# Six channels instead of four per chunk in the inverse stages of a frequency-domain MLP

## Chip, cores and metric

One NeuronCore of one Trainium2 chip runs the whole program. The metric is the device time of one execution in microseconds. Lower is better. Three runs of the kernel before are shown, and one further execution was profiled.

## The reference

The input `x` has 4 images of 128 x 128 pixels with 768 channels (NHWC, float32). Each image goes through a real 2-D FFT, the channels are cut into 8 blocks of 96, every frequency of a block goes through two complex layers, and the result is transformed back and added to `x`:

```python
xf = jnp.fft.rfft2(x, axes=(1, 2), norm='ortho')            # B, H, 65, 8 blocks, 96
o1r = relu(xr @ w1[0] - xi @ w1[1] + b1[0])
o1i = relu(xi @ w1[0] + xr @ w1[1] + b1[1])
o2r = o1r @ w2[0] - o1i @ w2[1] + b2[0]
o2i = o1i @ w2[0] + o1r @ w2[1] + b2[1]
o = softshrink(stack([o2r, o2i]), 0.01)
out = jnp.fft.irfft2(complex(o), s=(H, W), axes=(1, 2), norm='ortho') + x
```

Here `@` is the product within a block. All of it is float32.

## The kernel before, in words

**Units.** The work is cut into 32 units, one for each image and block of 96 channels. All FFTs are matrix products. A unit runs on TensorE (`body`, line 970) as stages: A (the forward transform along width, line 831), B (first layer, lines 846 and 863), C (forward transform along height, line 877), D (second layer, lines 894 and 900), then the inverse: E (along height, line 916) and F (along width, lines 926 to 928). D seeds and shrinks pass through VectorE and ScalarE. TensorE's order is written out by hand: the layers of unit n, with the first two groups (`AHEAD`) of A of unit n+1 inside; the inverse of unit n; the other 22 groups of A of unit n+1; and then the last `LATE` chunks of F of unit n, at line 976, just before the layers of unit n+1.

**The inverse of a unit.** It goes in 24 chunks (`NQ`) of 4 channels (`CHUNK`). Per chunk:

- E (`stage_e`): 4 float32 products of 128x128 by 128x128, one for each channel, into one bank of PSUM (512 float32 per partition). The trace has two records for each float32 product, so 8 records for a chunk.
- High part (ScalarE, line 607): a copy of the bank into `sums_high`, rounded to fp32r, 128x512.
- Low part (VectorE, line 773): bank minus high part into `sums_low`, 128x512. It frees the bank and signals `low_copied`.
- F (`stage_f`): six fp32r products. The 128 rows are cut in two slots, `F_SLOTS`, of 65 and 63; each slot gets high x high, low x high and high x low weights. With 4 channels they have 260 and 252 columns, and one record each. All six write one bank.
- Add (VectorE, `add`, lines 763 and 767): 0.5 x the pixels plus the middle of F's bank (96 rows, 384 elements), then the 32 "spread" rows (128 elements). It signals `f_added`.

E rotates over three banks (4, 5, 6), F over three (0, 1, 7), and the high and low parts over `RING` = 4 buffers. TensorE and VectorE both go in batches of two chunks: E, E, then F, F of the batch before; VectorE low, low, then add, add of the batch before. E(q) waits for low(q-3), F(q) for low(q) and, from q = 3 on, for add(q-3). VectorE's and ScalarE's orders are fixed by hand too, and each queue is first in, first out.

**Ends of the inverse.** The first E waits for the last shrink (line 720) and for the copy of the flip. After the 22nd F comes A of the next unit in banks 4 to 7; ScalarE and VectorE then evict A's groups. Late F (chunks 22 and 23) writes banks 2 and 3. The first B product (line 846) waits for ScalarE's gather at line 505, which comes after the evictions at line 551.

Of the kernel before, what the change touches and what calls it, by code (L numbers as in the profile page):

```python
# [10 lines left out]
ALU = mybir.AluOpType  # L11
ACT = mybir.ActivationFunctionType

IMAGES, SIZE, HIDDEN, BLOCKS = 4, 128, 768, 8
BLOCK = HIDDEN // BLOCKS
# [5 lines left out]
FW_EVEN, FW_ODD, FH, IH, IH_FIRST, FLIP_RE, FLIP_IM, IW_COS, IW_SIN = (slice(SIZE * i, SIZE * (i + 1)) for i in range(9))  # L21
# [20 lines left out]
THIRD = BLOCK // 3  # L42
SPREAD = SIZE // 4
# [1 line left out]
A_ROWS = 4  # L45

NA = TILE_ROWS // A_ROWS
CHUNK = 4
NQ = BLOCK // CHUNK
RING = 4  # L50

BATCH = 2

LATE = 2
NF = NQ - LATE

F_SLOTS = [(0, HALF + 1), (HALF + 1, SIZE)]
# [11 lines left out]
def group_rows(t, b):  # L69

    if t < NP:
        return [12 * t + 3 * i + b for i in range(A_ROWS)]
    return [j if j < TILE_ROWS else MIDDLE for j in (12 * t + 3 * i + 3 - b for i in range(A_ROWS))]
# [91 lines left out]
def fourier_mlp(nc, x, w1, b1, w2, b2, dft, out):  # L165
    with ExitStack() as ctx:
        def sb(name, shape, dtype=F32):
            return ctx.enter_context(nc.sbuf_tensor(name, shape, dtype))

        def sem(name):  # L170
            return ctx.enter_context(nc.semaphore(name))
# [9 lines left out]
        U = spectrum[:, :].rearrange("p (s j) -> p s j", j=PITCH)  # L181
# [13 lines left out]

        sums_high, sums_low = (sb(f"sums_{x}", [SIZE, RING, SIZE, CHUNK], F32R) for x in ("high", "low"))
        doubled = sb("doubled", [SIZE, FOLD_ROWS, SIZE])
# [14 lines left out]
        psum = ctx.enter_context(nc.psum_tensor("psum", [SIZE, 8, 512], F32))  # L212

        def bank(i, p=SIZE, n=512):
            return psum[0:p, i, 0:n]

        E_BANKS, F_BANKS = 3, [0, 1, 7]

        AHEAD = 2

        def bank_a(at):

            return bank(2 + at if at < AHEAD else (4, 7, 5, 6)[(at - AHEAD) % 4])

        def banks_b(s):

# [35 lines left out]

        def bank_e(q):

            return bank(4 + q % E_BANKS).rearrange("p (c h) -> p h c", h=SIZE)

        def bank_f(q):

            return bank(F_BANKS[q % len(F_BANKS)] if q < NF else 2 + q - NF).rearrange("p (h c) -> p h c", c=CHUNK)

        def spread_sums(q):

            first = bank_f(q)[:, 0]
            return bass.AP(first.tensor, first.offset, [first.ap[0], [(SIZE - SPREAD // 2) * CHUNK, 2], [CHUNK, SPREAD // 2], [1, CHUNK]])

        def spread_part(t, q):

            b, c = divmod(q * CHUNK, THIRD)  # L280
            second = (MIDDLE, MIDDLE + 2, MIDDLE + 1)[b]
            first = t[:, b, BLOCK + c:BLOCK + c + CHUNK]
            return bass.AP(first.tensor, first.offset, [first.ap[0], [(second - b) * SIZE, 2], [3 * SIZE, SPREAD // 2], [1, CHUNK]])

        x_loaded = [[sem(f"x_loaded{i}_{p}") for p in range(NP)] for i in range(2)]
        half_set, x_halved = sem("half_set"), sem("x_halved")
# [19 lines left out]
        e_done, high_copied, low_copied = sem("e_done"), sem("high_copied"), sem("low_copied")  # L306
        f_done, f_added, f_late_added = sem("f_done"), sem("f_added"), sem("f_late_added")
# [51 lines left out]
        def pairs(s):  # L359
            return 1 if GROUPS[s][1] is None else 2  # L360
# [133 lines left out]
        def _(act):  # L494
# [109 lines left out]
            def inverse(n):  # L604
                for q in range(NQ):
                    act.wait_ge(e_done, n * NQ + (q + 1))
                    act.activation(sums_high[:, q % RING], bank_e(q), ACT.Copy).then_inc(high_copied, 1)  # L607

# [19 lines left out]
        def _(dve):  # L628
# [23 lines left out]
            def unfold_step(n, par, k):  # L652
# [3 lines left out]
                if k == 0:  # L656
                    dve.wait_ge(f_added, n * NF + NF)
                    dve.wait_ge(f_late_added, n * LATE + LATE)

# [98 lines left out]
            def add(par, n, q):  # L758

                x_unit = xs[par]  # L760
                dve.wait_ge(f_done, n * NQ + (q + 1))
                part = x_unit[:, :, q * CHUNK:(q + 1) * CHUNK]
                dve.scalar_tensor_tensor(part, part, 0.5, bank_f(q)[:, SPREAD // 2:SIZE - SPREAD // 2], op0=ALU.mult, op1=ALU.add)
                part = spread_part(x_unit, q)
                if q == 0:
                    dve.wait_ge(x_halved, n + 1)
                dve.tensor_tensor(part, part, spread_sums(q), ALU.add).then_inc(f_added if q < NF else f_late_added, 1)

            def inverse(par, n):
                for batch in range(0, NQ, BATCH):  # L770
                    for q in range(batch, batch + BATCH):
                        dve.wait_ge(high_copied, n * NQ + (q + 1))
                        dve.tensor_tensor(sums_low[:, q % RING], bank_e(q), sums_high[:, q % RING],  # L773
                                          ALU.subtract).then_inc(low_copied, 1)
                    for q in range(batch - BATCH, batch):
                        if q >= 0:
                            add(par, n, q)

            def forward_next(n, m, par):

# [22 lines left out]
            for q in range(NF, NQ):  # L803
                add(1, UNITS - 1, q)
# [4 lines left out]
        def _(pe):  # L809
            def mat(columns):  # L810
                return mats[:, columns]

            def stage_a(m, par, n, first, end, end_of=None):
                for at, g in list(enumerate(A_ORDER))[first:end]:
                    if at % (NA // NP) == 0:
                        pe.wait_ge(x_folded[par], m * NFOLD + 2 * (at // (NA // NP) + 1))
                    if at >= AHEAD + 4:

                        if at % 2 == 0:
                            pe.wait_ge(act_copied, n * ACT_COPIES + (at // 2 - 1))  # L820
                        else:
                            pe.wait_ge(dve_copied, n * DVE_COPIES + (at // 2 - 1))
                    elif end_of is not None and at == AHEAD + 1:

                        pe.wait_ge(f_added, end_of * NF + (NF - 1))
                    elif end_of is not None and at >= AHEAD:

                        pe.wait_ge(low_copied, end_of * NQ + (NQ - 2 if at == AHEAD else NQ + at - AHEAD - 3))
                    for i, j in enumerate(group_rows(*g)):

                        last = pe.matmul(bank_a(at)[:, i * SIZE:(i + 1) * SIZE], xs[par][:, j, :],  # L831
                                         mat(FW_EVEN if g[0] < NP else FW_ODD), start=i == 0, stop=True, skip_group_check=True)
                        if j == MIDDLE:
                            last = pe.matmul(bank_a(at)[0:BLOCK, i * SIZE:(i + 1) * SIZE], xs[par][:, j, 0:BLOCK],
                                             mat(FW_EVEN), start=True, stop=True)
                    last.then_inc(a_done, 1)
# [31 lines left out]
            def stage_c(n, s):  # L868
                pe.wait_ge(b_copied, n * NS + (s + 1))
                if s == 1:  # L870

                    pe.wait_ge(f_late_added, n * LATE)
                for i in range(pairs(s)):
# [35 lines left out]
            def stage_e(n, q):  # L909
                if q == 0:  # L910
                    pe.wait_ge(shrunk, n * NS + NS)
                    pe.wait_ge(flip_copied, n + 1)
                if q >= E_BANKS:
                    pe.wait_ge(low_copied, n * NQ + (q - E_BANKS + 1))
                for i in range(CHUNK):
                    last = pe.matmul(bank_e(q)[:, :, i], U[:, q * CHUNK + i, 4:], mat(IH_FIRST if q * CHUNK < THIRD else IH), start=True, stop=True)  # L916
                last.then_inc(e_done, 1)

            def stage_f(n, q):
                pe.wait_ge(low_copied, n * NQ + (q + 1))  # L920

                if len(F_BANKS) <= q < NF:
                    pe.wait_ge(f_added, n * NF + (q - len(F_BANKS) + 1))
                for j, (lo, hi) in enumerate(F_SLOTS):
                    high, low, out = sums_high[:, q % RING, lo:hi], sums_low[:, q % RING, lo:hi], bank_f(q)[:, lo:hi]
                    pe.matmul(out, iw_high[:, j], high, start=True, stop=False)  # L926
                    pe.matmul(out, iw_high[:, j], low, start=False, stop=False)  # L927
                    last = pe.matmul(out, iw_low[:, j], high, start=False, stop=True)  # L928
                last.then_inc(f_done, 1)
# [25 lines left out]
                    stage_a(*ahead, 1, AHEAD)  # L955

            def inverse(n):
                for batch in range(0, NQ, BATCH):
                    for q in range(batch, batch + BATCH):
                        stage_e(n, q)  # L960
                    for q in range(batch - BATCH, batch):
                        if q >= 0:
                            stage_f(n, q)

            def late(n):
                for q in range(NF, NQ):
# [40 lines left out]
```

## Time and profile before

| what | us |
|---|---|
| median of 3 runs | 4921.51 |
| lowest and highest run | 4920.08, 4923.3 |
| profiled execution, its own time | 4919.26 |
| its span | 4917.5 |
| TensorE matmul busy | 4843.5 (98%) |
| VectorE busy | 3747.3 (76%) |
| ScalarE busy | 3015.9 (61%) |
| GpSimd busy | 1562.1 (32%) |
| granted TensorE clock, mean | 0.996 |

The profile comes from one execution. Busy time of an engine is the time in which it executes at least one instruction; TensorE's products are pipelined, so that one record lasts about 0.28 us while the next starts about 0.11 us later. The distance between starts is what a product costs, and the duration is what the next engine waits for. Weight loads have records of their own (PEld) and lie beside the products.

### The profile page before, as it was taken

What the parts mean: (1) busy time and instruction counts of PE and PEld (TensorE: products, weight loads), DVE (VectorE), ACT (ScalarE), POOL (GpSimd) and SP (SyncE); (2) the same over time, 40 slices, a digit from 0 to 9 for tenths busy, and PEclk for the clock granted to TensorE, in tenths of its full rate; (3) what the DMA queues carried; (4) which work ended last, traced back from release to release, by engine and by line L of the source; (5) the groups of instructions that cost most, each with busy time, mean ns of one, the idle gap of its engine ahead of it and who ended that gap; (6) DMA issues with size and microseconds to landing.
All of it is one profiled execution on the core that took longest, in us unless ns stands there. A gap on an engine that the chain in (4) does not pass through costs nothing.

```text
span 4917.5 us, 113473 instructions
## 1 busy us (share of the span) xinstructions
PE 4843.5 (98%) x40000; PEld 4707.5 (96%) x40000; DVE 3747.3 (76%) x5948; ACT 3015.9 (61%) x5428; POOL 1562.1 (32%) x1098
## 2 busy tenths in 40 slices
PE   8999999999999999999999999999999999999996
PEld 7999999999999999999999999999999999999996
DVE  5777777777777777777777777777777777777776
ACT  6655666556665556665566655666556666556653
POOL 3043223433234332244322343233433234332230
PEclk9999999999999999999999999999999999999998
DMA  5044423444333443334432344423444333443333
GB/s 118 19 96 109 102 60 75 91 109 106 68 72 88 103 107 78 73 83 96 109 85 64 83 96 109 98 65 75 91 109 104 70 75 84 103 107 80 70 78 90
DMA packets 1699713, 430.24 MB, mean 87 GB/s; under 512 B 1698848, under 2 KB 1698976, under 8 KB 1699104
## 3 DMA queue, kind: packets, MB, share of 16 engines
q1 hardware_dynamic: 1696768, 421.83, 38.7%
q8 instruction: 345, 5.65, 0.5%
q14 instruction: 264, 2.16, 0.2%
q10 hardware_dynamic: 2336, 0.59, 0.1%
HBM read 220.84 MB, written 201.33 MB: 86 GB/s over the span
## 4 chain that ended last, share of the span: by engine, by line
PE 97%; ACT 1%; issue 1%; SPq 1%; DVE 1%; DMA 0%; DVEq 0%; ACTq 0%
PE psum L846 15%; PE psum L877 14%; PE psum L900 14%; PE psum L916 14%; PE psum L831 13%; PE psum L863 8%; PE psum L894 7%; PE psum L926 4%; PE psum L927 4%; PE psum L928 4%; SPq L395 1%; PE psum L907 0%; PE psum L906 0%; DVE x L669 0%; DVE x L664 0%
## 5 line engine op out<-in xcount | busy, mean ns | idle before, releaser
L607 ACT ACTIVATE sums_high<-psum 128x512 fp32r<-128x512 f32 x768 | 458.1, 598 | 725.5 <-PE psum L916 725.4
L567 ACT ACTIVATE excess<-psum,over 128x768 f32<-128x768 f32 (+1 forms) x544 | 481.5, 885 | 579.4 <-PE psum L900 543.8
L846 PE MATMUL psum<-w_whole,whole 128*128 128x192 f32 x4160 | 802.0, 335 | 14.2 <-ACT whole L515 11.0
L900 PE MATMUL psum<-w2t,hidden 128*128 128x192 f32 x4160 | 763.2, 327 | 0.0
L846 PEld LDWEIGHTS psum<-w_whole,whole 128*128 128x128 f32 x4160 | 680.6, 196 | 83.8 <-issue 66.1
L916 PE MATMUL psum<-mats,spectrum 128*128 128x128 f32 x6144 | 747.5, 276 | 3.9 <-DVE sums_low L773 2.9
L877 PE MATMUL psum<-mats,mixed 128*128 128x128 f32 x6272 | 750.2, 275 | 0.0
L712 DVE COPY mixed<-psum 128x768 f32<-128x768 f32 (+1 forms) x512 | 475.1, 928 | 354.4 <-PE psum L846 312.8
L877 PEld LDWEIGHTS psum<-mats,mixed 128*128 128x128 f32 x6272 | 739.9, 192 | 1.2
L831 PE MATMUL psum<-mats,x 128*128 128x128 f32 x6144 | 706.2, 276 | 19.9 <-DVE x L648 19.8
L720 DVE SCALAR_TENSOR_TENSOR spectrum<-psum,excess 128x768 f32<-128x768 f32 (+1 forms) x512 | 481.4, 940 | 316.9 <-ACT excess L567 316.9
L916 PEld LDWEIGHTS psum<-mats,spectrum 128*128 128x128 f32 x6144 | 714.5, 192 | 8.8 <-DVE sums_low L773 4.1
L831 PEld LDWEIGHTS psum<-mats,x 128*128 128x128 f32 x6144 | 699.2, 193 | 20.6 <-issue 16.3
L773 DVE TENSOR_TENSOR sums_low<-psum,sums_high 128x512 fp32r<-128x512 f32 x768 | 530.1, 692 | 241.7 <-ACT sums_high L607 241.7
L900 PEld LDWEIGHTS psum<-w2t,hidden 128*128 128x128 f32 x4160 | 688.4, 190 | 7.2 <-issue 7.2
L444 POOL TENSOR_TENSOR x<-x 128x192 f32<-128x192 f32 x31 | 15.7, 505 | 1833.2 <-DMA x<-x 1833.1
L447 POOL TENSOR_TENSOR doubled<-x 128x640 f32<-128x640 f32 (+1 forms) x248 | 369.1, 1488 | 536.6 <-DMA x<-x 523.1
L734 DVE COPY psum<-b_rows 128x768 f32<-128x768 f32 (+1 forms) x544 | 504.5, 927 | 1.1
L863 PE MATMUL psum<-w_halved,halved 64*128 64x192 f32 x4160 | 463.3, 339 | 0.0
L926 PE MATMUL psum<-sums_high,iw_high 128*128 128x260 f32 (+1 forms) x1536 | 462.0, 301 | 0.0
L453 POOL TENSOR_TENSOR x<-x,doubled 128x640 f32<-128x640 f32 (+1 forms) x248 | 444.6, 1793 | 17.0
L894 PE MATMUL psum<-w2t,middle 64*128 64x192 f32 x4160 | 448.6, 326 | 0.8 <-DVE middle L725 0.8
(81 smaller groups left out, 7451.1 us busy)
## 6 DMA issues: line engine op xcount, KB each, us to landing
x<-x SPq DMA_DIRECT2D x736, 192.0 KB, 2.8
out<-x SPq DMA_DIRECT2D x736, 192.0 KB, 2.4
x<-x SPq DMA_DIRECT2D x736, 64.0 KB, 2.6
out<-x SPq DMA_DIRECT2D x736, 64.0 KB, 2.2
x<-x SPq DMA_DIRECT2D x32, 144.0 KB, 2.6
out<-x SPq DMA_DIRECT2D x32, 144.0 KB, 2.3
w2t<-L_conv_w SPq DMA_DIRECT2D x124, 36.0 KB, 1.8
x<-x SPq DMA_DIRECT2D x64, 48.0 KB, 2.3
```

Source lines behind the costliest of these rows:

```text
L567: act.activation(excess[:, :, 0:rows_d(t)], parts_d(t), ACT.Relu, bias=over[:, 0:1]).then_inc(excess_done, 1)
L720: dve.scalar_tensor_tensor(dst, parts_d(t), LAMBDA, excess[:, :, 0:rows], op0=ALU.add, op1=ALU.min).then_inc(shrunk, 1)
L734: dve.tensor_copy(bank_d(s).rearrange("p (k r) c -> p k r c", r=2)[:, 0:k], b2_rows[par][:, :, :].unsqueeze(1).broadcast_to([SIZE, k, 2, B ...
L773: dve.tensor_tensor(sums_low[:, q % RING], bank_e(q), sums_high[:, q % RING], ALU.subtract).then_inc(low_copied, 1)
L831: last = pe.matmul(bank_a(at)[:, i * SIZE:(i + 1) * SIZE], xs[par][:, j, :], mat(FW_EVEN if g[0] < NP else FW_ODD), start=i == 0, stop=Tru ...
L846: last = pe.matmul(bank_b(s, k), whole[s % 2][:, k // 2, :, k % 2], w1_whole[par][:, :, :].rearrange("p r o -> p (r o)"), start=opens and ...
L863: last = pe.matmul(bank_b(s, i + 2 * y), halved[s % 2][rows, :, i], w1_halved[par][rows, :, :].rearrange("p r o -> p (r o)"), start=opens ...
L877: last = pe.matmul(out[tile], flat[:, tile * SIZE:(tile + 1) * SIZE], mat(FH), start=True, stop=True)
L894: pe.matmul(sums_d(s, i + 2 * y), middle[s % 2][rows, i], w2_tile(par, rows, 1), start=False, stop=False, skip_group_check=True)
L900: last = pe.matmul(sums_d(s, k), hidden[s % 2][:, k // 2, k % 2], w2_tile(par, slice(0, SIZE), 2 * (k // 2)), start=False, stop=True, skip ...
L916: last = pe.matmul(bank_e(q)[:, :, i], U[:, q * CHUNK + i, 4:], mat(IH_FIRST if q * CHUNK < THIRD else IH), start=True, stop=True)
L926: pe.matmul(out, iw_high[:, j], high, start=True, stop=False)
```

## The change

`CHUNK` goes from 4 to 6, so the inverse of a unit has 16 chunks instead of 24. An E chunk is 6 products and takes a pair of banks (4 and 5, or 6 and 7). F's two slots have 390 and 378 columns; the first ends where one bank ends and the second begins the next bank. All F chunks but the last use the pair 0 and 1; the last one (`LATE` = 1) uses 2 and 3. The high and low parts have `RING` = 3 buffers of 768 elements per partition. Batches go: TensorE issues E(q), then F(q-2), and VectorE low(q), then add(q-1). E(q) waits for low(q-2), F(q) for low(q) and add(q-1). The spread part of an add is cut in two where its six channels cross a third of the block (chunks 5 and 10). The order of A's banks is 4, 5, 6, 7 instead of 4, 7, 5, 6.

```diff
--- before.py
+++ after.py
@@ -45,13 +45,13 @@
 A_ROWS = 4
 NA = TILE_ROWS // A_ROWS
-CHUNK = 4
+CHUNK = 6
 NQ = BLOCK // CHUNK
-RING = 4
-BATCH = 2
-LATE = 2
+RING = 3
+LEAD = 2
+LATE = 1
 NF = NQ - LATE
 F_SLOTS = [(0, HALF + 1), (HALF + 1, SIZE)]
@@ -216,13 +216,11 @@
-        E_BANKS, F_BANKS = 3, [0, 1, 7]
         AHEAD = 2
         def bank_a(at):
-            return bank(2 + at if at < AHEAD else (4, 7, 5, 6)[(at - AHEAD) % 4])
+            return bank(2 + at if at < AHEAD else 4 + (at - AHEAD) % 4)
         def banks_b(s):
@@ -264,23 +262,32 @@
         def bank_e(q):
-            return bank(4 + q % E_BANKS).rearrange("p (c h) -> p h c", h=SIZE)
+            flat = psum[:, 4 + 2 * (q % 2):6 + 2 * (q % 2), :].rearrange("p y n -> p (y n)")
+            return flat[:, 0:CHUNK * SIZE].rearrange("p (c h) -> p h c", h=SIZE)
         def bank_f(q):
-            return bank(F_BANKS[q % len(F_BANKS)] if q < NF else 2 + q - NF).rearrange("p (h c) -> p h c", c=CHUNK)
-        def spread_sums(q):
-            first = bank_f(q)[:, 0]
-            return bass.AP(first.tensor, first.offset, [first.ap[0], [(SIZE - SPREAD // 2) * CHUNK, 2], [CHUNK, SPREAD // 2], [1, CHUNK]])
-        def spread_part(t, q):
-            b, c = divmod(q * CHUNK, THIRD)
+            first, lo = 0 if q < NF else 2, 512 - F_SLOTS[0][1] * CHUNK
+            flat = psum[:, first:first + 2, :].rearrange("p y n -> p (y n)")
+            return flat[:, lo:lo + SIZE * CHUNK].rearrange("p (h c) -> p h c", c=CHUNK)
+        def spread_channels(q):
+            lo, hi = q * CHUNK, (q + 1) * CHUNK
+            cut = [lo] + [c for c in range(THIRD, BLOCK, THIRD) if lo < c < hi] + [hi]
+            return list(zip(cut, cut[1:]))
+        def spread_sums(q, lo, hi):
+            first = bank_f(q)[:, 0, lo - q * CHUNK:hi - q * CHUNK]
+            return bass.AP(first.tensor, first.offset, [first.ap[0], [(SIZE - SPREAD // 2) * CHUNK, 2], [CHUNK, SPREAD // 2], [1, hi - lo]])
+        def spread_part(t, lo, hi):
+            b, c = divmod(lo, THIRD)
             second = (MIDDLE, MIDDLE + 2, MIDDLE + 1)[b]
-            first = t[:, b, BLOCK + c:BLOCK + c + CHUNK]
-            return bass.AP(first.tensor, first.offset, [first.ap[0], [(second - b) * SIZE, 2], [3 * SIZE, SPREAD // 2], [1, CHUNK]])
+            first = t[:, b, BLOCK + c:BLOCK + c + hi - lo]
+            return bass.AP(first.tensor, first.offset, [first.ap[0], [(second - b) * SIZE, 2], [3 * SIZE, SPREAD // 2], [1, hi - lo]])
         x_loaded = [[sem(f"x_loaded{i}_{p}") for p in range(NP)] for i in range(2)]
         half_set, x_halved = sem("half_set"), sem("x_halved")
@@ -761,20 +768,20 @@
                 dve.wait_ge(f_done, n * NQ + (q + 1))
                 part = x_unit[:, :, q * CHUNK:(q + 1) * CHUNK]
                 dve.scalar_tensor_tensor(part, part, 0.5, bank_f(q)[:, SPREAD // 2:SIZE - SPREAD // 2], op0=ALU.mult, op1=ALU.add)
-                part = spread_part(x_unit, q)
                 if q == 0:
                     dve.wait_ge(x_halved, n + 1)
-                dve.tensor_tensor(part, part, spread_sums(q), ALU.add).then_inc(f_added if q < NF else f_late_added, 1)
+                for lo, hi in spread_channels(q):
+                    part = spread_part(x_unit, lo, hi)
+                    added = dve.tensor_tensor(part, part, spread_sums(q, lo, hi), ALU.add)
+                added.then_inc(f_added if q < NF else f_late_added, 1)
             def inverse(par, n):
-                for batch in range(0, NQ, BATCH):
-                    for q in range(batch, batch + BATCH):
-                        dve.wait_ge(high_copied, n * NQ + (q + 1))
-                        dve.tensor_tensor(sums_low[:, q % RING], bank_e(q), sums_high[:, q % RING],
-                                          ALU.subtract).then_inc(low_copied, 1)
-                    for q in range(batch - BATCH, batch):
-                        if q >= 0:
-                            add(par, n, q)
+                for q in range(NQ):
+                    dve.wait_ge(high_copied, n * NQ + (q + 1))
+                    dve.tensor_tensor(sums_low[:, q % RING], bank_e(q), sums_high[:, q % RING],
+                                      ALU.subtract).then_inc(low_copied, 1)
+                    if 1 <= q <= NF:
+                        add(par, n, q - 1)
             def forward_next(n, m, par):
@@ -820,12 +827,9 @@
                             pe.wait_ge(act_copied, n * ACT_COPIES + (at // 2 - 1))
                         else:
                             pe.wait_ge(dve_copied, n * DVE_COPIES + (at // 2 - 1))
-                    elif end_of is not None and at == AHEAD + 1:
-                        pe.wait_ge(f_added, end_of * NF + (NF - 1))
                     elif end_of is not None and at >= AHEAD:
-                        pe.wait_ge(low_copied, end_of * NQ + (NQ - 2 if at == AHEAD else NQ + at - AHEAD - 3))
+                        pe.wait_ge(low_copied, end_of * NQ + (NQ - 1 if at < AHEAD + 2 else NQ))
                     for i, j in enumerate(group_rows(*g)):
                         last = pe.matmul(bank_a(at)[:, i * SIZE:(i + 1) * SIZE], xs[par][:, j, :],
@@ -910,17 +914,17 @@
                 if q == 0:
                     pe.wait_ge(shrunk, n * NS + NS)
                     pe.wait_ge(flip_copied, n + 1)
-                if q >= E_BANKS:
-                    pe.wait_ge(low_copied, n * NQ + (q - E_BANKS + 1))
+                if q >= 2:
+                    pe.wait_ge(low_copied, n * NQ + (q - 1))
                 for i in range(CHUNK):
-                    last = pe.matmul(bank_e(q)[:, :, i], U[:, q * CHUNK + i, 4:], mat(IH_FIRST if q * CHUNK < THIRD else IH), start=True, stop=True)
+                    last = pe.matmul(bank_e(q)[:, :, i], U[:, q * CHUNK + i, 4:], mat(IH_FIRST if q * CHUNK + i < THIRD else IH), start=True, stop=True)
                 last.then_inc(e_done, 1)
             def stage_f(n, q):
                 pe.wait_ge(low_copied, n * NQ + (q + 1))
-                if len(F_BANKS) <= q < NF:
-                    pe.wait_ge(f_added, n * NF + (q - len(F_BANKS) + 1))
+                if 1 <= q < NF:
+                    pe.wait_ge(f_added, n * NF + q)
                 for j, (lo, hi) in enumerate(F_SLOTS):
                     high, low, out = sums_high[:, q % RING, lo:hi], sums_low[:, q % RING, lo:hi], bank_f(q)[:, lo:hi]
                     pe.matmul(out, iw_high[:, j], high, start=True, stop=False)
@@ -955,12 +959,11 @@
                     stage_a(*ahead, 1, AHEAD)
             def inverse(n):
-                for batch in range(0, NQ, BATCH):
-                    for q in range(batch, batch + BATCH):
+                for q in range(NF + LEAD):
+                    if q < NQ:
                         stage_e(n, q)
-                    for q in range(batch - BATCH, batch):
-                        if q >= 0:
-                            stage_f(n, q)
+                    if q >= LEAD:
+                        stage_f(n, q - LEAD)
             def late(n):
                 for q in range(NF, NQ):
```

## Rows read from the trace of the kernel before

**Rows 1.** The page: busy time of each engine, and the chain that ended last by engine.

```profile
PE 4843.5 (98%) x40000; PEld 4707.5 (96%) x40000; DVE 3747.3 (76%) x5948; ACT 3015.9 (61%) x5428; POOL 1562.1 (32%) x1098
...
PE 97%; ACT 1%; issue 1%; SPq 1%; DVE 1%; DMA 0%; DVEq 0%; ACTq 0%
```

**Rows 2.** Critical chain, a unit's inverse and after; columns start us, us, what.

```profile
148.19 1.78 PE psum L916 x16
...
173.74 1.78 PE psum L916 x16
...
176.94 19.69 PE psum L831 x176
...
208.75 1.30 PE psum L900 x8
```

**Rows 3.** Timeline of TensorE, three F triples of unit 0; columns start, duration, engine, line.

```profile
143.78 0.27 PE L926 MATMUL psum<-sums_high,iw_high 128*128 128x252 f32 x1
...
144.13 0.28 PE L926 MATMUL psum<-sums_high,iw_high 128*128 128x260 f32 x1
...
144.49 0.28 PE L926 MATMUL psum<-sums_high,iw_high 128*128 128x252 f32 x1
...
144.73 1.87 PEld L916 LDWEIGHTS psum<-mats,spectrum 128*128 128x128 f32 x16
144.84 1.95 PE L916 MATMUL psum<-mats,spectrum 128*128 128x128 f32 x16
```

**Rows 4.** Timeline of TensorE, the last two F triples of either width.

```profile
4881.09 0.28 PE L926 MATMUL psum<-sums_high,iw_high 128*128 128x252 f32 x1
...
4881.44 0.29 PE L926 MATMUL psum<-sums_high,iw_high 128*128 128x260 f32 x1
...
4881.80 0.28 PE L926 MATMUL psum<-sums_high,iw_high 128*128 128x252 f32 x1
```

**Rows 5.** Groups by line and shape: busy us, mean ns of one, idle before.

```profile
L773 DVE TENSOR_TENSOR sums_low<-psum,sums_high 128x512 fp32r<-128x512 f32 x768 | 530.1, 692 | 241.7 <-ACT sums_high L607 241.7
...
L607 ACT ACTIVATE sums_high<-psum 128x512 fp32r<-128x512 f32 x768 | 458.1, 598 | 725.5 <-PE psum L916 725.4
...
L720 DVE SCALAR_TENSOR_TENSOR spectrum<-psum,excess 128x768 f32<-128x768 f32 x480 | 457.1, 952 | 298.4 <-ACT excess L567 298.4
...
L567 ACT ACTIVATE excess<-psum,over 128x768 f32<-128x768 f32 x480 | 432.1, 900 | 504.2 <-PE psum L900 468.5 <-DVE spectrum L720 34.7
L763 DVE SCALAR_TENSOR_TENSOR x<-x,psum 128x384 f32<-128x384 f32 x768 | 419.6, 546 | 1.0
...
L557 ACT ACTIVATE hidden<-psum,b1t 128x256 f32<-128x256 f32 x512 | 242.1, 473 | 243.9 <-PE psum L877 243.9
...
L767 DVE TENSOR_TENSOR x<-x,psum 128x128 f32<-128x128 f32 x768 | 215.5, 281 | 0.0
```

**Rows 6.** Timeline of all engines where the inverse of unit 0 starts.

```profile
138.94 0.76 DVE L720 SCALAR_TENSOR_TENSOR spectrum<-psum,excess 128x576 f32<-128x576 f32 x1 [2.19 <-ACT excess L567]
...
139.75 2.87 PEld L916 LDWEIGHTS psum<-mats,spectrum 128*128 128x128 f32 x25
...
140.95 0.60 ACT L607 ACTIVATE sums_high<-psum 128x512 fp32r<-128x512 f32 x1 [1.65 <-PE psum L916]
141.58 0.69 DVE L773 TENSOR_TENSOR sums_low<-psum,sums_high 128x512 fp32r<-128x512 f32 x1 [1.88 <-ACT sums_high L607]
```

**Rows 7.** Critical chain at the end of the last unit: VectorE's adds back to back.

```profile
4881.49 0.46 DVE x L763
4881.96 0.20 DVE x L767
```

**Rows 8.** Busy time in one stretch of the inverse: PE, PEld, DVE, ACT, POOL, clock.

```profile
145.00:176.00 31.00, 31.00 (x275) 31.00 (x274) 26.29 (x59) 11.79 (x20) 0.00 (x0) 1.00 0.07 12
```

**Rows 9.** Timeline of ScalarE and TensorE where late F ends and B starts.

```profile
197.62 0.33 ACT L505 ACTIVATE whole<-spectrum 96x132 f32<-96x132 f32 x1
...
197.99 1.29 PEld L846 LDWEIGHTS psum<-w_whole,whole 128*128 128x128 f32 x8 [0.16 <-ACT whole L505]
```

## Prediction

> **What bounds the kernel now.** I read the page first. TensorE is busy 98% of the span and makes 97% of the chain that ended last; VectorE, ScalarE and GpSimd are busy 76%, 61% and 32% [rows 1]. So only two things change the time: what TensorE's own records cost, and gaps put between them. Busy time of the other engines matters only where TensorE must wait for it. The busy times by stretch show the inverse at its densest: in 31 us TensorE is busy for all 31.00, VectorE for 26.29, ScalarE for 11.79, GpSimd for none, at a granted clock of 1.00, which is 2.4 GHz [rows 8]. VectorE has the least slack there.
>
> The critical chain prices TensorE's records by the distance from one to the next. 16 E records (two E chunks of 4 channels) take 1.78 us, 0.1115 each. From the batch that ends its E at 148.19 + 1.78 to the one at 173.74 there are 8 batches in 25.55 us, 3.194 each [rows 2]; what is left for 12 F records is 1.41 us, 0.1177 each, 0.707 for an F chunk. F has on average 256 columns, 0.1067 us at 2.4 GHz, so an F record costs 11 ns above its columns.
>
> The timeline at the start of an inverse gives the latencies between engines. The first E's load starts 0.05 us after VectorE's shrink has ended (138.94 + 0.76, then 139.75). A load leads its product by 0.11 us (144.73 and 144.84 [rows 3]), so the first E takes effect at 139.86. Its 8 records are through at 140.75 and ScalarE starts at 140.95: 0.20 us from TensorE's last record to a waiting engine. VectorE starts 0.03 us after ScalarE ends [rows 6].
>
> **The change, part by part.** The profiled execution took 4919.26 us (span 4917.5), 2.2 under the median of 4921.51; the sum is made against the former and 2.2 added.
>
> *F's records.* Before, 22 chunks stand in the inverse: 22 x 0.707 = 15.55 us a unit. The new chunk has three records of 390 columns (162.5 ns) and three of 378 (157.5 ns), together 0.960 us, plus the six surcharges. At 11 ns each that is 1.026 us, and 15 chunks are 15.39: a gain of 0.16 us a unit. No row shows an fp32r record so long, so the surcharge is bounded. From below: a D record of 192 columns streamed twice (384) takes 1.30 / 8 = 0.1625 us [rows 2], only 2.5 ns over its 160. With that the chunk is 0.975 and the gain 0.93. From above: cost in proportion, 1.5 x 0.707 = 1.061, is a loss of 0.36. Steeper still, three F records of 252 columns take 0.35 us and three of 260 take 0.35 to 0.36 (first and last of 385 of each; their means are 0.346 and 0.360) [rows 3, 4]; drawn out from 8 columns to 130 more, that slope makes the chunk 1.14 and loses 1.6, which I leave outside the range. I take the fixed 11 ns, since it belongs to the same kind of record and the slope speaks against the cheaper one.
>
> The Trainium skill ("TensorE: Matmul & The Clock Gate", Back-to-back issue gap) gives N / 2.4 + 2.5 ns for a warm product. By that page F gains about 25 us over the kernel. The D record agrees with it, F before, at 11, doesn't.
>
> *Late F* shrinks from two chunks (1.41 us) to one (1.03). It frees nothing. The first B product already waits 0.16 us there for ScalarE's gather, which ends at 197.95, and its load starts at 197.99 [rows 9]; that chain starts from A's last groups, not from F. The wait grows to about 0.5 us, in place of F's 0.38. Cost 0. The shorter late add on VectorE, and A's new bank order, also cost 0: A's evictions cover them.
>
> *E* has the same 192 records, 21.4 us a unit. One chunk takes 12 x 0.1115 = 1.34 us.
>
> *High, low, add for six channels.* High: a copy of 512 takes 598 ns; ScalarE's slope from 256 (473) to 768 elements (900) is 0.834 ns each, so 768 take about 0.81 us, and at most the 0.90 of line 567. Low: 692 ns for 512 and 1.04 ns for each further element, 0.96, which the 952 of line 720 (768 elements in two banks) bears out [rows 5]. Add: VectorE starts the spread part 0.46 us after the main part and the next instruction 0.20 later [rows 7]. With 192 and 64 more elements the main part takes 0.46 + 0.20 = 0.66 and the spread part lasts 0.281 [rows 5] + 0.07 = 0.35: 1.01 us. In chunks 5 and 10 the split adds one start, 0.07. VectorE's total in a chunk of 2.37 us is 0.96 + 0.66 + 0.27 = 1.9, so it isn't full. ScalarE (0.81) hides. Reading two banks is what lines 720 and 567 do now. Nothing in the DMA queues moves, SP and POOL have no new step.
>
> *New wait 1, at E(2).* It needs low(0), where before E(3) did. From E(0) in effect at 139.86 in that unit: E(0) through at 141.20, high from 141.40 to 142.21, low from 142.24 to 143.20, load 143.25, product 143.36. E(1) is through at 142.54. **0.82 us** of TensorE idle. Behind it in the queue stand F(0) and everything else.
>
> *New wait 2, at F(14).* F has one pair of banks, so F(q) waits for add(q-1). After E(15) there is no E left: F(13), then F(14) at once. From F(13)'s end: 0.20 to VectorE, 1.01 for the add, 0.05 to the load, 0.11 to the product: **1.37 us** idle. Before, three banks took F(20) and F(21) without it.
>
> *New wait 3, at F(1) to F(13).* The same 1.37 us stands beside one E chunk of 1.34. Short by 0.03, 13 times, and by 0.07 more in the two split chunks: **0.53 us** a unit. Bounds: none, if the overlap is a few hundredths better; 0.9, if it is 0.03 worse each time. Low(q) behind add(q-2) on VectorE isn't late: from F(q-2)'s end it is done after 0.20 + 0.66 + 0.27 + 0.96 = 2.09 us, and E(q+2)'s load wants it after 1.37 + 1.03 - 0.11 = 2.29.
>
> The sum a unit: 0.82 + 1.37 + 0.53 - 0.16 = 2.56 us. In 32 units 81.9: 4919.3 + 81.9 + 2.2 = **5003 us**.
>
> What could hide these waits? Only idle in front of TensorE later in the unit, and that is the 0.16 us at B [rows 9], which comes from a chain counted from A and moves with it.
>
> **The rivals.** (a) F's surcharge falls to 2.5 ns. For it: the D record [rows 2]. Against it: F's own surcharge and slope [rows 3, 4]. 0.77 us a unit less, 5003 - 25 = 4978. The waits stay.
>
> (b) Wait 3 is larger: VectorE's round trip of 1.37 us is built from five short pieces, and 0.1 us more on it costs 13 x 0.1 x 32 = 42: 5045. VectorE's rows of 546 and 281 ns are steady, which speaks against it; that no row shows VectorE released by F does not exclude it.
>
> (c) The other side: faster. The mechanism is that an F record is paced by its weight load and not by its columns, so that wider records come free: 0.1177 us stay 0.1177, 15 chunks take 10.6, a gain of 4.9 a unit against 2.7 of waits: 5003 - 151 = 4852. The point from which it decides: F's chunk must fall under (15.55 - 2.72) / 15 = 0.855 us, 0.143 a record, while 390 columns alone are 0.1625 at the full clock and D's 384 cost just that. Very unlikely.
>
> (d) The waits don't appear, because bank or buffer reuse doesn't bind: then 5003 - 87 = 4916, within the noise of no change. The code names both semaphores and the rows have the durations, so hardly.
>
> **How the numbers follow.** About 0.2%, 10 us, is what a measurement here can tell from no change. Forecast 0.62, (a) 0.22, (b) 0.11, (c) 0.03, (d) 0.02. The range: down by (a), 25, and no wait 3, 17, to 4962; up by F in proportion, 17, high at 0.90, 3, and wait 3 at its bound, 12, to 5035, which I cut to 5032. Faster by over 0.2% is (c), 0.03; within 0.2% is (d), 0.02; slower 0.95.
>
> **What the profile afterwards would show.** TensorE idle before line 916 released by VectorE's line 773, once a unit, 0.8 us. Idle before line 926 released by line 767, once a unit 1.4 us and up to 13 times a few hundredths. F records 0.173 and 0.168 us apart; 0.165 and 0.160 mean (a). High 0.81, low 0.96, add's main part 0.75 and spread part 0.35 us. Line 846 waiting about 0.5 us for line 505. TensorE's share lower, the clock still 1.00. The prediction is wrong if line 926 is never released by VectorE, or if idle at line 926 in mid-inverse is over 0.1 us each.

## The result and the profile after

The changed kernel takes 5012.8 us (median of 4 runs, 5010.5 to 5014.9) against 4920.8. The ratio is 1.0188, with a 95% interval of 1.0175 to 1.0200. The change is slower, as forecast (5003 us, range 4962 to 5032), by 92 us in place of 82. The profiled execution took 5012.32 us with a span of 5010.1.

The page of the changed kernel, engines and chain, answers to [rows 1]:

```profile
PE 4876.9 (97%) x38464; PEld 4719.4 (94%) x38464; DVE 3683.8 (74%) x5244; ACT 2974.0 (59%) x5172; POOL 1554.4 (31%) x1098
...
PE 93%; ACT 2%; issue 2%; DVE 1%; SPq 1%; DMA 0%; ACTq 0%; DVEq 0%
```

TensorE has 1536 records fewer (38464; F's six per chunk, eight chunks fewer, in 32 units), yet it is busy 33 us longer and fills 97% of the span in place of 98%. Its share of the chain falls from 97% to 93%. The granted clock is still 1.00 in the inverse and 0.997 in the mean.

The groups by line and shape (busy us, mean ns of one, idle before) answer to [rows 5]. Lines 781, 614, 770 and 775 were 773, 607, 763 and 767:

```profile
L781 DVE TENSOR_TENSOR sums_low<-psum,sums_high 128x768 fp32r<-128x768 f32 x512 | 487.3, 952 | 93.9 <-ACT sums_high L614 93.8
...
L614 ACT ACTIVATE sums_high<-psum 128x768 fp32r<-128x768 f32 x512 | 416.3, 813 | 807.6 <-PE psum L920 807.6
...
L770 DVE SCALAR_TENSOR_TENSOR x<-x,psum 128x576 f32<-128x576 f32 x512 | 386.5, 755 | 295.1 <-PE psum L932 294.1
...
L775 DVE TENSOR_TENSOR x<-x,psum 128x192 f32<-128x192 f32 x448 | 155.9, 348 | 0.0
```

Low takes 952 ns (0.96 expected), high 813 (0.81), the add's main part 755 and its spread part 348. VectorE now waits 294 us in all for F at line 770; the same line had 1.0 us of waiting before [rows 5].

The waits (who waited for whom: us in total, times, longest):

```profile
DVE x L770 <- PE psum L932: 294.1, 480, 1.9
...
PE psum L930 <- DVE x L775: 35.9, 32, 1.2
...
PE psum L920 <- DVE sums_low L781: 19.8, 32, 1.1
```

TensorE waits once a unit at E (line 920) for a low part and once a unit at F (line 930) for an add. The totals, 19.8 and 35.9 us, understate these two: a record goes on for 0.16 us or more after the next one could have started, and that much of each gap is booked as busy. The critical chain shows them whole. First the start of the inverse of unit 0 (columns: start, duration, what):

```profile
140.63 1.51 PE psum L920 x12
...
142.16 0.82 ACT sums_high L614
...
143.01 0.97 DVE sums_low L781
143.98 0.04 issue
144.02 1.60 PE psum L920 x12
```

E(0)'s last record ends at 142.14 and ScalarE starts at 142.16; then come high 0.82, low 0.97, and E(2)'s load at 144.02. Its product takes effect 0.11 us later, at 144.13. E(0) took effect at 140.64 (its last record's end, less the record's 0.275 and eleven distances of 0.1115), so two chunks were through at 143.32: a gap of 0.81 us (0.82 in the forecast).

Then the middle of the inverse, one period:

```profile
149.11 1.34 PE psum L920 x12
150.45 0.22 PE psum L930
150.67 0.18 PE psum L931
150.85 0.18 PE psum L932
151.03 0.18 PE psum L930
151.21 0.17 PE psum L931
151.38 0.17 PE psum L932
151.55 1.34 PE psum L920 x12
```

One period is 151.55 - 149.11 = 2.44 us. The first of F's six records takes 0.22 us and the others 0.17 to 0.18. The timeline of the same place shows why:

```profile
151.21 0.33 PE L932 MATMUL psum<-sums_high,iw_low 128*128 128x378 f32 x1
...
151.58 0.76 DVE L770 SCALAR_TENSOR_TENSOR x<-x,psum 128x576 f32<-128x576 f32 x1 [0.55 <-PE psum L932]
...
152.25 0.35 DVE L775 TENSOR_TENSOR x<-x,psum 128x192 f32<-128x192 f32 x1
...
152.66 0.19 PEld L930 LDWEIGHTS psum<-sums_high,iw_high 128*128 128x128 f32 x1
```

F(2)'s last record ends at 151.54, VectorE starts at 151.58, its spread part ends at 152.60, and the load of F(3) starts 0.06 us after that. The low part that F(3) also needs, low(3), stands before this add in VectorE's queue, so it is the add that F(3) waits for last. No row of the waits names this: the gap is shorter than what a record's end hides. It can be read only from the distance between records.

And the end of the inverse:

```profile
178.24 0.18 PE psum L932
...
178.45 0.06 DVE x L770
...
179.12 0.36 DVE x L775
...
179.52 0.45 PE psum L930
```

F(13)'s last record ends at 178.42. F(14)'s load starts at 179.52, when the add is done. Unhindered, F(14)'s first record would have ended at 178.60; it ended at 179.52 + 0.45 = 179.97. That is a gap of 1.37 us, with no E left to fill it.

From the first E of unit 0 to that of unit 1 the kernel before takes 151.12 us (139.86 to 290.98) and the changed one 154.14 (140.63 to 294.77): 3.02 us a unit, and the inverse itself 40.21 in place of 37.08, 3.13 more.

### The profile page after: what moved, and what is told of

Read it like the earlier page. It is cut to its first block, busy times and chain, and to the rows that moved or that the text cites. A ratio compares the mean times of both kernels' runs of the same rounds, so it can differ in the third digit from the quotient of the medians.

```text
span 5010.1 us, 108315 instructions
## 1 busy us (share of the span) xinstructions
PE 4876.9 (97%) x38464; PEld 4719.4 (94%) x38464; DVE 3683.8 (74%) x5244; ACT 2974.0 (59%) x5172; POOL 1554.4 (31%) x1098
## 4 chain that ended last, share of the span: by engine, by line
PE 93%; ACT 2%; issue 2%; DVE 1%; SPq 1%; DMA 0%; ACTq 0%; DVEq 0%
PE psum L850 15%; PE psum L881 14%; PE psum L904 14%; PE psum L920 13%; PE psum L835 12%; PE psum L867 8%; PE psum L898 7%; PE psum L930 4%; PE psum L932 3%; PE psum L931 3%; DVE sums_low L781 1%; ACT spectrum L551 1%; ACT spectrum L558 1%; SPq L402 1%; ACT sums_high L614 1%
## 5 line engine op out<-in xcount | busy, mean ns | idle before, releaser
L614 ACT ACTIVATE sums_high<-psum 128x768 fp32r<-128x768 f32 x512 | 416.3, 813 | 807.6 <-PE psum L920 807.6
L920 PE MATMUL psum<-mats,spectrum 128*128 128x128 f32 x6144 | 769.2, 276 | 20.8 <-DVE sums_low L781 19.8
L920 PEld LDWEIGHTS psum<-mats,spectrum 128*128 128x128 f32 x6144 | 747.4, 191 | 30.5 <-DVE sums_low L781 25.8
L770 DVE SCALAR_TENSOR_TENSOR x<-x,psum 128x576 f32<-128x576 f32 x512 | 386.5, 755 | 295.1 <-PE psum L932 294.1
L781 DVE TENSOR_TENSOR sums_low<-psum,sums_high 128x768 fp32r<-128x768 f32 x512 | 487.3, 952 | 93.9 <-ACT sums_high L614 93.8
L455 POOL TENSOR_TENSOR x<-x 128x640 f32<-128x640 f32 (+1 forms) x248 | 454.7, 1833 | 0.0
```

## The experiments

Two theories stood against each other. One is the ledger: three separate waits and dearer F records, each with its own price. The other is the rival: the loss is in the two-bank chunks or the change of order as such, or the waits only hand their time on, so that removing one brings nothing. The base is the changed kernel (5012.8 us) unless another is named, and the unit's length is read as above.

**1. F(14) later.** TensorE issues F(14) behind the next unit's A groups 2 and 3, which need only low(14). The cut below is TensorE's part. VectorE does its add after the evictions of groups 1 and 3.

```diff
-                stage_a(m + par, 1 - par, n + 1, AHEAD, NA, end_of=n)
+                stage_a(m + par, 1 - par, n + 1, AHEAD, AHEAD + 2, end_of=n)
+                stage_f(n, NF - 1)
+                stage_a(m + par, 1 - par, n + 1, AHEAD + 2, NA, end_of=n)
```

> The changed kernel, with F(14) put behind the next unit's A groups 2 and 3 on TensorE, and its add on VectorE put behind the evictions of A groups 1 and 3. If the wait at F(14) is a cost of its own (1.37 us a unit): it disappears in 31 units, 5013 - 42 = 4971 us. If it only moves (VectorE's evictions come late and A group 7 waits for its bank): 0.5 to 1.4 us a unit come back there, 4985 to 5013.

Measured: 4977.1 us, ratio to the kernel before 1.0118 (1.0101 to 1.0135). That is 36 us less. The critical chain, where the inverse ends:

```profile
179.08 1.78 PE psum L837 x16
180.86 0.18 PE psum L932
...
181.92 15.37 PE psum L837 x136
```

The two A groups (16 records in 1.78 us) cover the add's round trip, and F(14)'s first record takes 0.18 us, the same as its neighbours: the gap is gone. From F(13) to F(14) and A the unit gains 1.37 us. But the unit is 152.93 us long, 1.21 less and not 1.37. The other 0.16 comes back inside A: its 136 records take 15.37 us, where 152 took 16.98 in the changed kernel, 0.1117 each, so that 15.19 was to be expected. VectorE now has the add between its evictions, which would make the next of them later. That this is the cause was not shown; it fits experiment 5, where the shorter add takes the 0.16 away. So the ledger holds here, and a tenth of the gain is handed on.

**2. Adds without their spread part** (line 775 is left out; the 32 spread rows get no sum).

```diff
-                for lo, hi in spread_channels(q):
-                    part = spread_part(x_unit, lo, hi)
-                    added = dve.tensor_tensor(part, part, spread_sums(q, lo, hi), ALU.add)
```

> The changed kernel without the spread part of the adds (32 of the 128 rows of a pixel column block get no sum). If F(1) to F(13) wait because VectorE's add is slightly longer than one E chunk: the add's signal comes 0.26 us earlier, the 13 waits (0.6 us a unit together) go and the one at F(14) falls from 1.37 to 1.1, in all 0.85 us a unit, 5013 - 27 = 4986 us. If low(q), queued behind the add, is what E and F really wait for in mid-inverse, or if these gaps are only the cost of going from E to F records: nothing of the 0.6, and 5013 - 8 = 5005.

Measured: 4978.1 us, ratio 1.0117 (1.0101 to 1.0134); 35 us less in place of 27. The unit is 153.20 us long, 0.94 less. One period in mid-inverse:

```profile
150.19 1.34 PE psum L917 x12
151.52 0.18 PE psum L927
...
152.58 1.34 PE psum L917 x12
```

The period is 2.39 us and the first F record takes 0.18. Over twelve periods the mean is 2.389 (147.80 to 176.47), against 2.441 in the changed kernel (146.69 to 175.98, with both split chunks): 0.052 us, 13 times, is 0.68 us a unit. The wait at F(14) fell by 0.26 (its total in the waits from 35.9 to 27.5 us, in 32 units). Together that is 0.94, all that this unit gained, and 30 of the 35 us over 32 units; some 3 more lie in the last four units (see "The sum" below). The run alone would not tell add from low, since without the spread parts low comes earlier too. The place does: the gap stood before F's first record and not before E's, and F(q) finds low(q) done before add(q-1). The add's round trip was the wait.

**3. High and low of chunk 0 in two pieces.** The first four channels go through ScalarE and VectorE while E still works on the last two. TensorE's and ScalarE's parts of the edit are shown; VectorE's is like ScalarE's.

```diff
+                    if q == 0 and i == 3:
+                        last.then_inc(e_part, 1)
...
+                    if q == 0:
+                        act.wait_ge(e_part, n + 1)
+                        act.activation(sums_high[:, 0, :, 0:4], bank_e(0)[:, :, 0:4], ACT.Copy).then_inc(high_part, 1)
+                        act.wait_ge(e_done, n * NQ + 1)
+                        act.activation(sums_high[:, 0, :, 4:], bank_e(0)[:, :, 4:], ACT.Copy).then_inc(high_copied, 1)
+                        continue
```

> The changed kernel, with the high and low parts of chunk 0 taken in two pieces (channels 0 to 3 after E's fourth product, then 4 and 5). If E(2) waits for the round trip through ScalarE and VectorE: low(0) ends at 2.75 + 0.1 us after E(0) starts and not at 3.34, the wait shrinks from 0.82 to 0.22 us a unit, 5013 - 19 = 4994 us. If the next wait (E(3) for low(1), or F(0)) takes it over: 5013.

Measured: 4997.0 us, ratio 1.0154 (1.0137 to 1.0171), 16 us less. The chain at the start:

```profile
139.75 4.42 PE psum L933 x36
144.17 0.18 PE psum L945
...
145.22 1.34 PE psum L933 x12
```

36 E records now run as one group of 4.42 us, with no step through ScalarE or VectorE between them. 36 x 0.1115 and the 0.16 us that a last record lasts on would be 4.17, so 0.25 us of waiting is left. The unit is 153.56 us, 0.58 less (0.60 expected). E(3) and F(0) don't take the wait over.

**4. Both edits, 1 and 3.** No new lines.

> The changed kernel with F(14) moved behind two groups of A and chunk 0 in two pieces, both edits of the two runs before together. If the waits at F(14) and at E(2) are separate costs: 5013 - 36 - 16 = 4961 us. If one covers for the other: 4975 to 4980.

Measured: 4960.8 us, ratio 1.0084 (1.0067 to 1.0101). The two are separate costs, and they add up as expected. This is the best version with six channels and all of the computation, and it is still 41 us slower than the kernel before.

**5. All three edits** (the spread part of the adds left out).

> Both edits, and the spread part of the adds left out, so that F never waits for an add. If the ledger is complete: 4961 - 13 x 0.052 x 32 = 4939 us, still above the kernel before by F's dearer records (0.24 us a unit), 0.25 at E(2) and 0.16 in A, 21 in all. If records of 390 and 378 columns were a gain that the waits hid: below 4920.

Measured: 4929.6 us, ratio 1.0021 (1.0011 to 1.0030), 9 us better than expected and still above the kernel before. The chain at the end of the inverse:

```profile
173.58 1.34 PE psum L932 x12
...
175.97 1.78 PE psum L847 x16
...
178.81 15.20 PE psum L847 x136
```

The period is 2.39 us as in experiment 2. A's 136 records take 15.20 us: the 0.16 that came back in experiment 1 is gone too, probably because VectorE, without the spread parts, is earlier at its evictions (0.16 x 31 = 5 us of the 9). Another 3 us lie in the last four units: there a unit took 0.9 us more than elsewhere in experiment 4 and takes 0.1 more here (see "The sum" below). The unit is 151.53 us, 0.41 above the kernel before. F's records account for 0.24 of it and the rest of the wait at E(2) for 0.25, less 0.11 by which the part of the unit outside its inverse is shorter. Without any wait on an add, with less work on VectorE, the six-channel version doesn't win: the waits hid no gain.

**6. The order alone.** The kernel before, with three banks each for E and F and four channels, but in the new order without batches.

```diff
-                for batch in range(0, NQ, BATCH):
-                    for q in range(batch, batch + BATCH):
-                        stage_e(n, q)
-                    for q in range(batch - BATCH, batch):
-                        if q >= 0:
-                            stage_f(n, q)
+                for q in range(NQ):
+                    stage_e(n, q)
+                    if q >= 2:
+                        stage_f(n, q - 2)
```

VectorE's loop is changed in the same way.

> The kernel before (4 channels, three banks each for E and F), with the order of the changed one: TensorE E(q), F(q-2), VectorE low(q), add(q-2), no batches. If the loss comes from the number of banks and the size of the chunks: as the kernel before, 4920 us, within 10. If going from E to F records after every chunk has a price of its own (0.05 us twice as often as before would be 24 x 0.05 x 32 / 2 = 19): 4935 to 4945.

Measured: 4922.3 us over 10 runs, ratio 1.0005 (0.9995 to 1.0014): no difference that the times show. In the traces a unit takes 151.20 us in place of 151.12. So going from E to F after each chunk costs next to nothing, 0.08 us a unit. What is left for the loss is the size of the chunks and the number of them in flight, which the change moved together.

**7. What an F record costs.** Two runs cut F's columns, and leave out the rest of the sums.

```diff
-                for j, (lo, hi) in enumerate(F_SLOTS):
+                for j, (lo, hi) in enumerate([(0, 33), (HALF + 1, HALF + 1 + 32)]):
```

> The changed kernel, F's products over 33 and 32 of the 65 and 63 rows (198 and 192 columns; the rest of the sums is left out). What an F record costs: in proportion to columns, 0.46 ns each as at 252 to 390 columns, 0.091 and 0.088 us; with a fixed surcharge of 11 to 17 ns, 0.093 to 0.1; paced by the weight load below about 256 columns, 0.1115 for both. VectorE's low(q) then ends after E(q+2) wants it, so that TensorE waits for line 781 in mid-inverse, 0.1 to 0.3 us each; about 4880 to 4900 us.

> The changed kernel, F's products over 50 and 48 rows (300 and 288 columns; the rest of the sums is left out). F's record in proportion to its columns, 0.46 ns each: 0.138 and 0.132 us. With the surcharge of 17 ns that the changed kernel shows: 0.142 and 0.137. With the 11 ns of the kernel before: 0.136 and 0.131.

The timeline of the first of them, in one F chunk, records of 198 and then 192 columns (start, duration, engine, line):

```profile
151.49 0.27 PE L931 MATMUL psum<-sums_low,iw_high 128*128 128x198 f32 x1
151.60 0.28 PE L932 MATMUL psum<-sums_high,iw_low 128*128 128x198 f32 x1
151.71 0.27 PE L930 MATMUL psum<-sums_high,iw_high 128*128 128x192 f32 x1
151.82 0.28 PE L931 MATMUL psum<-sums_low,iw_high 128*128 128x192 f32 x1
```

They start 0.11 us apart, though 198 columns take 0.0825 at 2.4 GHz. The table has the distances from start to start, as means over all F chunks that the trace shows whole. For the wider slot it is the way from a chunk's second record to its fourth, halved, and for the narrower one that from the fourth to the sixth, halved, over 509 chunks or more. The first record of a chunk is left out: its recorded start lies before the records ahead of it are through.

| columns | distance, ns | columns at 2.4 GHz, ns | above | ns per column |
|---|---|---|---|---|
| 192, 198 | 111, 112 | 80, 82.5 | 31, 29 | 0.58, 0.56 |
| 252, 260 (before) | 116, 119 | 105, 108 | 11 | 0.46 |
| 288, 300 | 134, 138 | 120, 125 | 14, 13 | 0.466, 0.459 |
| 378, 390 (changed) | 174, 178 | 157.5, 162.5 | 17, 15 | 0.461, 0.455 |

From 252 columns up an F record costs about 0.46 ns a column. Below, it is held at about 0.11 us, the distance that E's records and their loads have too. Neither a fixed 11 nor a fixed 17 ns fits: 300 columns should then take 136 or 142, and 252 columns 116 or 122; they took 138 and 116. A line through the outermost two, 252 and 390 columns, has 0.45 ns a column and 2 ns beside, so a small fixed part isn't ruled out. The time of the kernel with 192 and 198 columns, 4854 us in one run, was further down than the 4880 to 4900 expected; its E groups in mid-inverse took 1.38 to 1.56 us in place of 1.34, a smaller wait for low than I had reckoned with. The kernel with 288 and 300 columns took 4902 us in one run.

**8. The two banks.** The changed kernel, with F's six products alternating between the two banks.

```diff
+                for k in range(3):
+                    for j, (lo, hi) in enumerate(F_SLOTS):
...
+                        weights, moving = ((iw_high, high), (iw_high, low), (iw_low, high))[k]
+                        last = pe.matmul(out, weights[:, j], moving, start=k == 0, stop=k == 2)
```

> The changed kernel with F's six records alternating between its two banks (the order of the six products only). If the 17 ns that an F record costs above its columns come from three records in a row adding onto the same bank: 0.163 to 0.166 us a record, a chunk of 0.98 instead of 1.05 and 1 us a unit less, 5013 - 34 = 4979 us. If they belong to fp32r records as such: the same 0.175 and 5013 us.

Measured: 5016.0 us, ratio 1.0194 (1.0177 to 1.0211), against 1.0188 (1.0175 to 1.0200) for the changed kernel: no difference. The critical chain:

```profile
149.52 1.10 PE psum L932 x6
150.61 1.34 PE psum L920 x12
```

F's six records take 1.10 us with the wait in front, as before, and in the timeline the wide and the narrow ones start 177 and 174 ns apart, as in the changed kernel. Adding onto the same bank three times in a row isn't what makes them dear. Why an fp32r record costs 0.46 ns a column, while D's float32 records of 384 come at 0.423 [rows 2], stays open.

## Why the prediction was right, point by point

**The bound.** Right: TensorE's records and the gaps between them made the whole difference. No other engine became the bound.

**New wait 1, at E(2).** Forecast 0.82 us a unit, read 0.81; experiment 3 removed 0.58 of it.

**New wait 2, at F(14).** Forecast 1.37, read 1.37; experiment 1 removed it and 36 us with it.

**New wait 3, at F(1) to F(13).** Mechanism right, size short: 0.53 forecast, 0.68 measured by experiment 2. Round trip and cover differ by a few hundredths of a microsecond, and each hundredth counts 13 x 32 times, 4.2 us. Rival (b), this wait larger by 0.1 us each time, had the direction but not the size: it was larger by about 0.01. The time that the prediction gives for it, 5045, lay outside its own range.

**F's records.** This is the term that was mis-sized. I took "the fixed 11 ns, since it belongs to the same kind of record" and so a gain of 0.16 us a unit. A chunk cost 1.05 us (the period of 2.389 without waits, less E's 1.34), in proportion to its columns within 1%, and F lost 15 x 1.05 - 15.51 = 0.24. (The 15.51 is F's share of the inverse before: 37.08, less 192 x 0.1115 for E and the 0.16 that a last record lasts on.) So the term had the wrong sign, and the upper bound, a price in proportion, was nearer. The two widths of the kernel before already leant that way: their slope is steeper than 2.4 GHz allows. I named it and used it only against the lower end. Drawn out over 130 columns that slope gave 1.14 us a chunk, which was too much: widths of 252 and 260 lie too close together to fix a slope. Rival (a), from the Trainium skill ("TensorE: Matmul & The Clock Gate", Back-to-back issue gap), would have 0.165 us for 390 columns; the trace has 0.178, so that for fp32r records of this kernel the rule doesn't hold. It does hold for D's. (The page gives it for an isolated product; D's and F's come in a stream.) The prediction's "about 25 us" for that page is the distance from its own forecast; against the kernel before, its gain of 0.93 us a unit would be 30.

**The sum.** Waits 2.86 and F 0.24 are 3.10 us a unit; the inverse grew by 3.13. The whole unit grew by 3.02, since the rest of it is 0.11 shorter. The forecast had 2.56. At 3.02 a unit, 32 units would be 97 us, and the two profiled executions differ by 93. Two things at the loop's ends, which the prediction didn't look at, make the difference.

First, four units are one turn of the loop, and at six turns TensorE waits anyway. In the kernel before, the B and the E that follow cost 3.2 us more there than in other units; in the changed kernel it is 1.8. So 8 us of what the inverse loses are made up there, by a path that was not followed. The prediction said that only the 0.16 us at B could hide the waits; here it was wrong, and this error offset about half of the 18 us by which the terms for F and wait 3 fell short. Without it the changed kernel would have taken about 5021 us, so that the closeness of the sum owes something to luck.

Second, the last four units stand outside the loop, and there wait 3 is larger. The critical chain of the last unit but one:

```profile
4791.37 1.34 PE psum L920 x12
...
4793.87 1.34 PE psum L920 x12
```

The period is 2.50 us in place of 2.44. The load of F's first record starts 0.12 us after the add's end, where inside the loop it is 0.05 (medians). In the kernel of experiment 2 the period is 2.39 in both places. Why the hand-over is longer there stays open.

**What was costed at nothing.** Late F's shorter time was indeed lost to the gather on ScalarE. The timeline of the changed kernel at this point:

```profile
201.49 0.32 ACT L512 ACTIVATE whole<-spectrum 96x132 f32<-96x132 f32 x1
...
201.86 1.29 PEld L850 LDWEIGHTS psum<-w_whole,whole 128*128 128x128 f32 x8 [0.62 <-ACT whole L512]
```

TensorE's load waits 0.62 us there, in place of 0.16 [rows 9]. From A's first record to B's first the two kernels take the same, 21.2 us. The new order cost next to nothing (experiment 6). High, reading two banks and the add's main part took what the rows of before had said.

**Rivals (c) and (d).** Wide records didn't come free, and both semaphores did bind. The change bought 48 F records fewer a unit, which are worth nothing when a record is paid by the column (as in the table of experiment 7 from 252 columns up), and paid for them with two E chunks in flight in place of three and one F chunk in place of three.

## What to carry to other kernels

Before fewer, wider instructions are counted as a gain, look whether their price has a fixed part at all: two widths that lie well apart give the slope, and if slope times width is the whole price there is nothing to win. Larger chunks in the same PSUM mean fewer of them in flight; cost the round trip of the first one, of the last one, and of the steady state, each against the TensorE work that can stand beside it, because the ends can lose more than the middle (here 2.18 us a unit against 0.68). A repeated gap of some hundredths of a microsecond appeared here in no view of waits; it had to be read from the distance between records. And a cost per unit is to be checked on more than one unit: those at a loop's turn and behind the loop came out differently here, by 8 us one way and by some 3 the other.

## What the runs showed of the hardware

An fp32r product with a weight load of its own cost about 0.46 ns a column (0.455 to 0.466), at a granted clock of 1.00, from 252 to 390 columns. With 378 and 390 columns it was the same with three records in a row on one bank and alternating between two. With 192 and 198 columns the distance stayed at 0.111 and 0.112 us, which is what float32 records with a weight load of 128 columns take in E. And alternating between float32 and fp32r records after every chunk, in place of every second, changed the time by no more than 10 runs can tell (ratio 0.9995 to 1.0014).
